# A recurrent block's TensorE order: two pairs of thin products side by side, the pair of k and r behind the projection of v

## The reference

```python
xa = _ln(x, ln1_w, ln1_b)
sx = concatenate([state[:, 1:2] - xa[:, :1], xa[:, :-1] - xa[:, 1:]], axis=1)
xxx = tanh((xa + sx * maa_x) @ maa_w1).reshape(b, l, 5, 32)
xxx = einsum('blfd,fde->blfe', xxx, maa_w2)
xm = xa[:, :, None] + sx[:, :, None] * (maa_stack + xxx)
xk, xw, xv, xr, xg = (xm[:, :, j] for j in range(5))
w = exp(-exp(time_decay + tanh(xw @ td_w1) @ td_w2))
r = xr @ Wr.T;  k = xk @ Wk.T;  v = xv @ Wv.T;  g = silu(xg @ Wg.T)
# per token and head: out = r (u * k v + s);  s = k v + w * s
og = group_norm(out) * gn_w + gn_b
x1 = x + og * g @ Wo.T
xc = _ln(x1, ln2_w, ln2_b);  xk2, xr2 = shifted mixes of xc
return x1 + sigmoid(xr2 @ Wfr.T) * (square(relu(xk2 @ Wfk.T)) @ Wfv.T)
```

## Time and profile before

| | |
|---|---|
| median of 3 runs | 3761.22 us |
| profiled execution, whole | 3760.67 us |
| its span | 3758.9 us |
| mean granted TensorE clock | 0.932 |
| recurrent block, 1757 to 2743 us: PE, DVE, ACT, POOL busy | 884, 733, 280, 492 us of 986 |
| steps 4 to 8, 1920 to 2400 us: PE, DVE, ACT, POOL busy | 452, 383, 143, 251 us of 480 |

### The profile page before, as it was taken

One profiled execution on the slowest core, in us unless ns is written; L12 is line 12 of the kernel. 1 busy time (PEld: TensorE's weight loads), 2 busy tenths in 40 slices (PEclk: granted clock), 3 DMA queues, 4 the chain that ended last, 5 costly groups with the idle time before them and its releaser, 6 DMA issues. The chain is left out here.

```text
span 3758.9 us, 52788 instructions
## 1 busy us (share of the span) xinstructions
PE 3346.7 (89%) x19344; PEld 2226.2 (59%) x19344; DVE 1773.3 (47%) x2532; ACT 1121.8 (30%) x4036; POOL 857.7 (23%) x574
## 2 busy tenths in 40 slices
PE   7998789979999877776899999999689999989999
PEld 5565455546667445454677777777445555466765
DVE  4554355520000375764678788787734546410000
ACT  2434233321111344442232332322223433311111
POOL 2333133310000001001555555555400000000000
PEclk9999899989999888897899898998889999989999
DMA  3110131110000131101111111110013101010000
GB/s 152 41 40 25 60 130 51 37 51 23 22 14 14 43 136 42 47 19 48 40 38 36 34 45 34 34 44 26 25 65 120 41 24 36 20 42 20 31 33 11
DMA packets 103587, 168.87 MB, mean 45 GB/s; under 512 B 16432, under 2 KB 53936, under 8 KB 100016
## 3 DMA queue, kind: packets, MB, share of 16 engines
q1 hardware_dynamic: 98576, 123.27, 10.3%
q10 hardware_dynamic: 4896, 44.04, 2.8%
HBM read 133.72 MB, written 33.55 MB: 44 GB/s over the span
## 5 line engine op out<-in xcount | busy, mean ns | idle before, releaser
L1704 POOL TENSOR_TENSOR rec_S<-rec_S,rec_r_t 128x1024 f32<-128x1024 f32 x128 | 309.8, 2420 | 322.9 <-DVE rec_S L1984 322.9
L1984 DVE TENSOR_TENSOR_SCAN rec_S<-rec_decay,rec_S 128x1024 f32<-128x1024 f32 x128 | 318.3, 2487 | 29.5 <-ACT rec_S L1774 25.0
L1390 PE MATMUL mlp_bank<-mlp_src_t,region_a 128*128 128x256 f32 x1024 | 225.4, 383 | 1.7 <-ACT mlp_src_t L1315 1.7
L1390 PE MATMUL pmlp_bank<-pmlp_src_t,region_a 128*128 128x256 f32 x1024 | 225.3, 382 | 1.3 <-ACT pmlp_src_t L1315 1.3
L1402 PE MATMUL pmlp_bank<-region_a,pmlp_h_t 128*128 128x512 f32 x512 | 221.1, 592 | 0.0
L1402 PE MATMUL mlp_bank<-region_a,mlp_h_t 128*128 128x512 f32 x512 | 221.1, 592 | 0.0
L547 ACT ACTIVATE group_scores<-group_scores,group_negmax 128x128 f32<-128x128 f32 x512 | 197.4, 391 | 77.8 <-DVE group_negmax L737 66.6
L1390 PEld LDWEIGHTS mlp_bank<-mlp_src_t,region_a 128*128 128x128 f32 x1024 | 196.6, 192 | 32.4 <-issue 5.5
L1390 PEld LDWEIGHTS pmlp_bank<-pmlp_src_t,region_a 128*128 128x128 f32 x1024 | 196.5, 192 | 31.9 <-issue 5.0
L1360 DVE TENSOR_TENSOR mlp_y<-mlp_bank,mlp_xres 128x512 f32<-128x512 f32 x16 | 11.1, 692 | 381.0 <-PE mlp_bank L1402 381.0
L1360 DVE TENSOR_TENSOR pmlp_y<-pmlp_bank,pmlp_xres 128x512 f32<-128x512 f32 x16 | 11.1, 691 | 371.4 <-PE pmlp_bank L1402 371.4
(11 more groups left out here) (325 smaller groups left out, 6652.9 us busy)
## 6 DMA issues: line engine op xcount, KB each, us to landing
rec_vb<-v_by_head SPq DMA_DIRECT2D x32, 512.0 KB, 4.3
region_a<-in_C_w ACTq DMA_DIRECT2D x2, 4096.0 KB, 19.8
region_a<-in_G_w ACTq DMA_DIRECT2D x2, 4096.0 KB, 19.5
self_x<-in_x SPq DMA_DIRECT2D x16, 256.0 KB, 3.4
self_xres<-in_x SPq DMA_DIRECT2D x16, 256.0 KB, 2.6
rows_A<-self_xres SPq DMA_DIRECT2D x16, 256.0 KB, 2.0
cross_x<-rows_A SPq DMA_DIRECT2D x16, 256.0 KB, 3.3
cross_ctx_t<-in_ctx_t SPq DMA_DIRECT2D x16, 256.0 KB, 3.3
```

The lines of the kernel that those rows point to most:

```text
L1390: product = nc.tensor.matmul(ph.bank(item)[:, i * TT:(i + 1) * TT], W1[:, c, f:f + 128], src_t[:, c, :, :], start=c == 0, stop=c == C - 1)
L1704: nc.gpsimd.tensor_tensor(S[u % 4][:, :, :], S[u % 4][:, :, :], bcast(r_t[:, s.k, UNITS[u][0], :], [128, JH, T], 1), ALU.mult)\
L1984: nc.vector.tensor_tensor_scan(St[:, :, :].rearrange(flat), decay[m][:, :, :].rearrange(flat), St[:, :, :].rearrange(flat), 0.0, ALU.mult, ...
```

## The change

Nothing is added to the computation and nothing is taken from it. The order of instructions changes on four engines, and two pairs of mixes are issued alternately.

- TensorE: a new `mix_pair(s, f, g)` waits until all five tanh are done ("mx" free), and then issues the products of both mixes in turn, chunk by chunk. Mixes 1 and 2 become a pair right behind `low_rank` and `sum_heads(back, 7)`. Mixes 0 and 3 become a pair that stands between the two halves of `out_rows`, behind the projection of v. The second half of `ffn_gate` moves from the end of the step to the next step, behind the first pair; the halves of `ffn_values` move behind `sum_heads(middle, 0)` and behind `variance`. `sum_heads` of units 3, 4 and 5, the transposes x2 and mix 4 move between whole projections.
- ScalarE: `sigmoid_tanh` moves from the end of the step to the next one, ahead of `squares`.
- GpSimd: `add_rows` of mixes 0, 3 and 4 each stand one `multiply_states` later.
- VectorE: `mix` of 0, 3 and 4 each stand one unit later, and `output` one unit earlier.

```diff
         banks = StepBanks("rec", sem, {b: ps(f"bank_{b}", [128, BANK]) for b in "abcdn"}, [
-            ("a", "mx", 0), ("d", "fv", 3), ("b", "mix1", 0), ("n", "mean", 2),
+            ("a", "mx", 0), ("b", "mix1", 0), ("a", "mix2", 0), ("n", "mean", 2),
...
@@ GpSimd @@
                 if middle:
                     multiply_states(middle, 2)
+                if middle:
+                    multiply_states(middle, 3)
                 if front:
                     add_rows(front, 0)
-                if middle:
-                    multiply_states(middle, 3)
-                if front:
-                    add_rows(front, 3)
                 if back:
                     rsqrt(back, stats2, rstd2, back_norm[2], rstd2_done)
                 if middle:
                     multiply_states(middle, 4)
                 if front:
+                    add_rows(front, 3)
+                if middle:
+                    multiply_states(middle, 5)
+                if front:
                     add_rows(front, 4)
-                if middle:
-                    multiply_states(middle, 5)
@@ ScalarE @@
                     make_decay(middle, 3)
+                if tail:
+                    sigmoid_tanh(tail)
                 if back:
                     squares(back)
...
-                if back:
-                    sigmoid_tanh(back)
@@ VectorE @@
                     scan(middle, 2)
-                if front:
-                    mix(front, 0)
                 if back:
                     gated(back)
+                if tail:
+                    output(tail)
                 if middle:
                     inputs(middle, 3)
                     scan(middle, 3)
                 if front:
-                    mix(front, 3)
-                if tail:
-                    output(tail)
+                    mix(front, 0)
...
@@ TensorE @@
+            def mix_pair(s, f, g):
+
+                for item in (f, g):
+                    begin(s, f"mix{item}")
+                freed(pe, s, "mx")
+                for c in range(C):
+                    for item in (f, g):
+                        tile, p0 = MIX_TILE[item]
+                        last = nc.tensor.matmul(banks.bank(f"mix{item}")[:, c * 128:c * 128 + 128],
+                                                mix_w[p0:p0 + 64, tile, c * 128:c * 128 + 128],
+                                                low[tile][p0:p0 + 64, :], start=True, stop=True)
+                        if c == C - 1:
+                            done(f"mix{item}", last)
...
+                if front:
+                    mix_pair(front, 1, 2)
+                if tail:
+                    ffn_gate(tail, 1)
...
-                    mix(front, 0)
                     project(front, "v", 2, 0)
                     project(front, "v", 2, 1)
...
-                    mix(front, 3)
+                    mix_pair(front, 0, 3)
...
                 if back:
                     ffn_gate(back, 0)
-                    ffn_gate(back, 1)
```

More of the change, by code:

```diff
@@ L1745, in step @@
                 if front:
-                    add_rows(front, 3)
+                    add_rows(front, 0)
                 if back:
@@ L2106, in step @@
                 if front:
-                    mix(front, 4)
+                    mix(front, 3)
                 if middle:
```

26 lines of the change are left out of this document (11 added, 15 removed), and 9 rows, old and new, of the table banks.

## The result

| | before | after |
|---|---|---|
| median | 3762.15 us (5 runs, 3760.19 to 3766.33) | 3783.87 us (5 runs, 3780.34 to 3787.85) |
| ratio | | 1.0057 (1.0042 to 1.0072) |
| profiled execution, its span | 3760.67, 3758.9 us | 3787.85, 3786.1 us |
| mean of steps 3 to 14 | 57.78 us | 58.55 us |
| single steps 3 to 14 | 56.4 to 58.1 us | 55.8 to 61.5 us; steps 5, 7, 9 and 13 take 55.8 to 56.1 |

The account below looks back on a forecast made before the run. TensorE, partly at half clock, and VectorE, with 47.0 us work and 11.0 waits, bound the step. 13 steps gain 0.8 each, 10 us; first steps lose 6: -4, so 3757 us, own range 3747 to 3768, overall 3728 to 3782.

Parts of the forecast that it names:

- the forecast: Whole kernel: steps of 57.0 us and 6 us lost at the start, 3757 us in all; chance 0.42.
- full step at full clock: Recurrent block: a step takes 55.6 us if the clock stays up, 2.2 below the mean of 57.78.
- step 15 and the steps without a front: End of the recurrent block: step 15 gains 0.8 us, steps 16 to 18 keep their time.
- The chain at full clock: Full step, followed from the end of make_gate: VectorE's waits 9.66 us plus work 46.0 us.
- the new wait of 2.7 us: VectorE ahead of mix_back: waits 2.75 us, where before it had no wait; the largest new term.
- the granted clock: TensorE at low_rank's end and ahead of sum_heads 4: falls worth 3.4 us in four steps of ten, 1.4 per step.
- the term for the first steps: Steps 0 to 2: +4, +2.5 and -0.5 us, 6 us lost; bounds 0 and +10.
- the pair at the start: Steps 0 and 1: the pair of mixes 1 and 2 waits for all tanh, +1.1 us.
- The second one: Rival: clock falls once or more in nearly each step, at low_rank's end or ahead of sum_heads 4; 3783 us; chance 0.26.
- The first rival: Full steps: the clock stays up, 22 us less, 3739 us; chance 0.2.
- The third: Rival: wait ahead of mix_back absent or short, clock stays up; 52 us less, 3709 us; chance 0.08.
- the fourth: Rival: the pair's products run one after the other, step 58.8 us, 3780 us; chance 0.04.

Follow-up runs that it names:

- TensorE's order restored: Changed kernel with mix 4 and half of r ahead of sum_heads 4, and transposes x2 behind r, as before the change; 3774.89 us, ratio 1.0034.
- the late adds alone: Change's first-half kernel (3705.06 us), with only VectorE's and GpSimd's orders from the full change: mix and add_rows of 0, 3, 4 one unit later; 3756.83 us, ratio 0.9989.
- The filled gap: Changed kernel with the second half of k's products issued twice, 1.9 us of dense work ahead of sum_heads 4; 3754.09 us, ratio 0.998.
- mix 0 ahead of v: Changed kernel with mix 0 ahead of v on TensorE and mix 3 alone in the second pair's place; 3773.80 us, ratio 1.0036.
- the first half: Kernel before plus only the pair of mixes 1 and 2, feed-forward halves between thin products, and sigmoid a step later; 3705.06 us, ratio 0.9853.
- the kernel without the pair: The first half of the change alone, but with mixes 1 and 2 issued one after the other; 3704.90 us, ratio 0.9851.
- two buffers: Changed kernel with a second mixtmp, add_rows 0 and 3 ahead of rsqrt and multiply_states 4, sum_heads 4, x2, mix 4 as before the change; 3708.91 us, ratio 0.9861.

## Why the prediction was wrong

Against the profiled execution before, the forecast was -4 us, and the profiled one after is +27 (+22 by the medians). By the terms of the sum:

| term | predicted | measured |
|---|---|---|
| full step at full clock | 55.6 | 55.97 |
| low clock, per step, steps 5 to 14 | 1.4 | 58.27 - 55.97 = 2.3 |
| the same, steps 3 to 14 | 1.4 | 58.55 - 55.97 = 2.6 |
| steps 3 to 14 in all, to before | -9.4 | +9.2 |
| steps 0 to 2 | +6 | +18.2 |
| step 15 and the steps without a front | -0.8 | -3.3 |
| untouched blocks | 0 | +3.1 |

**The chain at full clock was right.** VectorE's waits, predicted and in the step shown: mix 1 2.79, with 0.45 more in the scan ahead of it (3.08, and the scan takes 2.52 instead of 2.28), the mean 0.34 (0.34), the variance 1.02 (1.04), mix 0 0.79 (0.73), mix_back 2.75 (2.74), the last scan 0.36 (0.37). TensorE's idle times too: 1.2 ahead of the pair (1.19), 1.0 ahead of v (1.05), 0.65 ahead of sum_heads 2 (0.54), 2.2 ahead of sum_heads 4 (2.08). The moves cost and gave what they were worked out to, but for 0.4 us a step. That the new wait of 2.7 us eats the gain was thus known from the profile of before, and so was its path: scan 4, rsqrt and multiply_states 4, sum_heads 4, x2, mix 4 and r. What the prediction doesn't have is the second path to r right behind that one, by way of add_rows 3. It matters for the remedy: with TensorE's order restored the wait stays, with the late adds alone it is back, and it goes when both paths are shortened.

**The step that failed is "the granted clock", and with it the term for the first steps.** Forecast and profile differ by 31 us. Some 14 of them are the low clock in steps 3 to 14 (2.6 a step instead of 1.4), 12 the first steps, 4 the step at full clock, and 3 code that the change doesn't touch; the last steps give 2.5 back. For the clock the prediction took the shorter stretch of the earlier trace rows, 3.4 us, in four steps of ten. Both places it named did fall, low_rank's end and the idle time ahead of sum_heads 4, and the size of one fall was near: steps 10 and 11, with a single one, take 59.1, so 3.15 each. But the stretch is 6.8 us long, and there were six of them in ten steps (6, 8, 10, 11, 12, 14), 1.9 us a step. One fall at low_rank and three within v, behind the 1.05 us of idle time ahead of it, make the other 0.4. The prediction had counted that idle time among the waits and not among the risks. Nor does it list the 1.8 to 2.1 us for which TensorE waits ahead of low_rank, behind which the falls at low_rank begin. The steps just behind the start were worse: steps 3 and 4 together take 5.9 us more than the forecast's 57.0 each. The filled gap shows directly that it was the clock: the wait of mix_back stayed, and ten steps became 18.7 us shorter.

**The first steps** took 18 us more and not 6. Step 0 was near (+4 predicted, +4.6 measured): k starts 1793.04 - 1766.70 = 26.3 us into it, where the earlier trace rows have 1782.08 - 1760.3 = 21.8. Steps 1 and 2 were not (+2.5 and -0.5 against +7.0 and +6.7). There the low clock grew from 12.7 to 16.7 and from 14.6 to 23.3 us; at half speed that is worth up to 2.0 and 4.4 of it. With mix 0 ahead of v steps 0 to 2 lose 10.7 us of the 18.2; the late adds alone lengthen steps 1 and 2 by 1.8 and 3.0. For the pair at the start the prediction had +1.1 in step 0; with it and without it (the first half against the kernel without the pair) that step takes 40.7 and 38.1 us, so it costs 2.6. The prediction gave step 2 a saving of 0.5; that step has no tail, and so no fv and fr to stand between the thin products. That this is why its saving is missing is argued and not shown. TensorE at step 0's k, in the changed kernel:

```profile
1782.76 6.38 PE L2183 MATMUL rec_bank_b<-rec_xm,region_a 128*128 128x128 f32 x32 [1.24 <-ACT rec_e_t L1820]
...
1793.04 3.84 PE L2183 MATMUL rec_k<-rec_xm,region_a 128*128 128x128 f32 x32 [2.00 <-POOL rec_xm L1696]
```

v waits 1.24 for the exponential and k 2.00 for add_rows, with nothing between them but the pair; most of v is at half clock.

**The rivals.** The second one, falls in nearly every step and 3783 us, is the one whose mechanism came true. It and the forecast differed only in how often the clock falls; it had nearly every step, and eight of twelve had a fall. That its time agrees to 1 us is partly luck: its 13 steps were to lose 16 us, and steps 3 to 14 lost 9, while the first steps lost three times the 6 it had for them. The first rival's figure would have needed a clock that stays up. The filled gap comes near its steps (seven of ten at 55.8 to 56.0), but five of its twelve full steps still fall elsewhere and its steps 0 to 2 are 16 us longer than before, so it takes 3754 and not 3739. The third is excluded by the wait of 2.7, and the fourth by the 1.10 us in which both mixes stand.

**The gaps and the rule on them.** In the kernel before, 1.72 us of idle time went with a fall in each full step, in the changed one 2.01 to 2.77 us in eight of twelve, and in the late adds alone 1.55 to 1.73 us in eight of twelve. In the first half alone, where no idle time of TensorE in a full step is over 1.2 us, none fell. But such a length is no limit either: the 1.05 us ahead of v went with a fall in three of twelve steps of the changed kernel and in five of twelve with two buffers. The Trainium skill, "TensorE: Matmul & The Clock Gate", section "Why this matters for your kernels", puts its limit for idle gaps above all of these. By that rule the changed kernel would have stayed at 55.97 us a step; the trace disagrees, by 2.6 us a step over steps 3 to 14.

What stays open is which steps fall. The idle time ahead of sum_heads 4 is 2.09 us in steps 11 and 13, one with a fall and one without, step 14 falls with 2.01, and filling another gap made the falls more frequent, not fewer. That the fall goes when this gap is filled is shown. What makes it come in one step and not in the next was not settled.

## What to carry to other kernels

Work out the chain of waits at full clock, and then treat each idle time that TensorE has between thin products as a place where the clock may fall. In the versions of this kernel idle times of 1.6 to 3.0 us went with a fall in six to twelve of the twelve full steps, and some of 1.05 us did too. Independent dense work in that very gap is the cure that was shown here. When an engine's helper operation is moved later, follow its result through the single buffer to the last consumer: mixes 0, 3 and 4 and their add_rows one unit later cost 52 of 57 us here. When a wait has two paths of nearly one length, mending one of them shows nothing: with TensorE's order for r restored, the wait of 2.7 us stayed. Issuing two products side by side is worth nothing when the pair must wait for the later of its inputs by as much as it saves.

## What was not expected of the hardware

- Useless work made the kernel faster: 16 more records of dense products in each step, and 3754.09 us instead of 3783.87.
- Filling an idle time elsewhere made it slower: with fr ahead of the pair, 3797.88 us, as the clock fell ahead of r in ten steps of twelve, behind an idle time that in several of them had not grown (2.07 or 2.08 us), and at low_rank in six.
- Blocks that no kernel here touched moved by some us: the first low_rank starts between 1758.5 and 1767.5 us over the twelve kernels. The kernels were profiled once each, so no run tells whether that comes from the kernel or from the execution. A change of a few us in the sum can't be read from one profiled execution of each.
